# Node statistics and router sums on ScalarE and GpSimd inside the group stage, and the second MLP bias as one bf16 product

## The chip, the core and the metric

One NeuronCore of a Trainium2 chip runs the whole kernel. The metric is the device time of one launch in microseconds (us). The engines are named as the profile names them: PE is TensorE (PEld its weight loads), DVE is VectorE, ACT is ScalarE, POOL is GpSimd, SP is SyncE, which here only issues transfers. A name with q (POOLq) is the engine's instruction queue: loads of registers, branches, arithmetic on addresses.

## What is computed

One layer over a graph of 12500 nodes with 256 features each and 212500 edges:

```python
xn = _layernorm(x)
x = x + gnn(xn, weight, edge_weight, src, dst) + mix(xn, ...)
x = x + ffn(_layernorm(x), wr, br, w1, b1, w2, b2)

# gnn: out[src] += edge_weight * (xn @ weight)[dst]
# mix: linear attention over all nodes, x1 = layer_norm(t + xn) * g1 + b1n, then
#      h = gelu(x1 @ W1.T + b1);  y = h @ W2.T + b2;  layer_norm(y + x1) * g2 + b2n
# ffn: weights = x @ wr + br;  the 6249 nodes of largest weight:
#      y = (gelu(sel @ w1 + b1) @ w2 + b2) * weight, added to their rows
```

Two things of it matter here. The bias b2 of the mix's second matrix product (with the first layer norm's own bias added to it), and, between the two lines that set x, the mean and variance of each node's row and its product with wr, the router sum: without them no node can be normalised or chosen.

## The kernel before

The nodes are 98 tiles of 128 rows (NT = 98). The sum that becomes x stands in SBUF as `acc`, 256 columns to a tile. The edges come in 128 blocks of 1664 (NSB = 128).

In the main part, each block permutes and expands its edges on TensorE (L948 is the expansion, in bf16), ScalarE moves the result from PSUM to `rowbuf`, and GpSimd scatters it to DRAM, sorted by the tile that it is to be added to. Beside the blocks runs the mix: at first the attention's sums, and in later blocks the mixing of two tiles (49 times, in a pattern of two blocks with mixing and one without). Of one mixing, `mlp_down` is TensorE's last part: for each of two tiles the product with W2 (L1004, f32), x1 times a diagonal matrix (L1007), and the bias (L1009), then VectorE takes the statistics of the result (L1701). VectorE's step of a block begins at L1665, when TensorE has done the block before.

Then comes the group stage. The sorted rows are cut into groups of 256 that belong to one tile each, and tiles follow each other in order. A step has 8 groups (RG = 8), in four pairs k; 112 steps were made. For each pair SyncE loads its rows (L584), VectorE makes four one-hot matrices with the edge weights (L1822), TensorE multiplies them with the rows (L1082), ScalarE moves the sums to SBUF (L1341), and GpSimd adds them to the tile: it loads the tile's place from the row of group buckets (L725), waits for ScalarE and for its own last add (L726, L727), and adds (L728). Each buffer is given back by counting semaphores. The order on each engine is the order of the program.

Behind the last add stands the statistics loop: VectorE takes seven tiles at a time, their statistics (L1841), their product with wr into `prod` (L1843), and aggregates (L1848, L1850); ScalarE sums each product over its columns with an accumulator (L1348). Then VectorE works out the inverse square roots (`inv_sqrt`, from L1396), the router weights and the choice of nodes, and in the end comes the FFN over the chosen rows.

## Time and profile before

| | us |
|---|---|
| median of 3 runs | 3774.55 (3771.11 to 3775.57) |
| the profiled execution | 3799.59 |
| its span | 3797.8 |
| the stretch of mixing, by the bias products | 1284 to 2257 |
| the group stage's adds | 2354 to 3211 |
| the statistics loop | 3213 to 3291 |
| selection and FFN | from 3291 |

A profile is of one execution, and here that one took 0.7% longer than the median. Durations are read from it. The timeline gives the start, the length, engine, line and operation, what is written and read, how many follow each other, and in brackets how long the engine was idle before and what ended that. The chain is the sequence of work that ended last, followed back from the last instruction; a step is on it if the next one waited for it. An engine's busy share tells little where the stages have different limits: what a change in one stage is worth is read from the waits and the chain of that stage.

### The profile page before, as it was taken

To read this page: it belongs to the slowest core of one execution; us is meant where nothing else is said; L and a number is where in the kernel's file an instruction comes from. 1 tells how busy PE (TensorE), PEld (TensorE's weight loads), DVE (VectorE), ACT (ScalarE), POOL (GpSimd) and SP (SyncE) were. 2 spreads that over 40 slices of the span, in tenths; PEclk is the share of its full clock that TensorE was granted. 3 is DMA by queue.
4 is the path that set the end of the run, shared out by engine and by line. 5 is a ranking of instruction groups with operands and counts; after the bars stand their busy time and mean duration, and the time that the engine had idled before them with its cause. 6 is when DMAs were issued, how large, how long until landed. Compare 5 with 4: busy or idle time off the path is not lost.

```text
span 3797.8 us, 81728 instructions
## 1 busy us (share of the span) xinstructions
PE 3073.4 (81%) x18820; PEld 2305.1 (61%) x18820; DVE 2599.6 (68%) x6591; ACT 1555.3 (41%) x3781; POOL 2113.8 (56%) x2304
## 2 busy tenths in 40 slices
PE   3777738888888788888888886999999997029998
PEld 2444426666666666666676664777777775018887
DVE  6888884444444677777787773999999999861111
ACT  4444404555555444444444443333333333673222
POOL 1445534555555566666666565777777776003433
PEclk7899969999999999999899898999999999559999
DMA  5777727787777766666677666888888887161111
GB/s 162 239 262 261 256 73 239 263 261 254 252 264 262 237 229 217 216 215 222 222 228 231 203 211 221 272 278 276 277 276 277 277 277 229 62 217 50 54 52 44
DMA packets 427482, 818.33 MB, mean 215 GB/s; under 512 B 45499, under 2 KB 203191, under 8 KB 427256
## 3 DMA queue, kind: packets, MB, share of 16 engines
q1 hardware_dynamic: 348376, 559.80, 48.5%
q0 software_dynamic: 78880, 256.49, 17.7%
q14 instruction: 203, 1.66, 0.1%
q8 instruction: 23, 0.38, 0.0%
HBM read 459.96 MB, written 356.17 MB: 215 GB/s over the span
## 4 chain that ended last, share of the span: by engine, by line
PE 38%; issue 14%; DVE 14%; POOL 13%; ACT 6%; another core or an unknown queue 6%; DMA 3%; POOLq 3%; SPq 1%; DVEq 1%; ACTq 0%
POOL acc L728 13%; PE ps L948 12%; PE ps L1135 5%; PE ps L1125 5%; PE ps L961 3%; PE ps L995 2%; ACT rowbuf L1261 2%; POOLq L725 2%; PE ps L1082 2%; PE ps L1004 2%; DVE acc L1490 2%; PE ps L957 1%; DMA rowbuf<-sorted_rows 1%; DMA acc<-bucket_rows 1%
## 5 line engine op out<-in xcount | busy, mean ns | idle before, releaser
L695 POOL DMA_INDIRECT sorted_rows<-rowbuf,posu x896 | 1003.4, 1120 | 768.2 <-ACT rowbuf L1261 554.3
L948 PE MATMUL ps<-mainbuf 128*128 128x256 bf16 x5376 | 731.5, 280 | 195.7 <-ACT rowbuf L1261 140.5
L1082 PE MATMUL ps<-rowbuf,mainbuf 128*128 128x256 f32 x3584 | 844.7, 392 | 25.9 <-DVE mainbuf L1822 20.9
L1822 DVE TENSOR_SCALAR mainbuf<-cols,rowbuf 128x128 f32<-128x128 f32 x1792 | 820.9, 528 | 58.5 <-DMA rowbuf<-sorted_rows 50.2
L728 POOL TENSOR_TENSOR acc<-acc,node 128x256 f32 x896 | 673.3, 751 | 196.3 <-POOL acc L728 156.1
L1082 PEld LDWEIGHTS ps<-rowbuf,mainbuf 128*128 128x128 f32 x3584 | 620.3, 189 | 250.1 <-DVE mainbuf L1822 177.5
L948 PEld LDWEIGHTS ps<-mainbuf 128*128 128x128 bf16 x5376 | 502.2, 100 | 338.8 <-ACT rowbuf L1261 187.7
L1261 ACT ACTIVATE rowbuf<-ps 128x512 f32<-128x512 f32 x896 | 515.4, 594 | 447.2 <-PE ps L948 371.5
L1341 ACT ACTIVATE node<-ps 128x512 f32<-128x512 f32 x448 | 267.6, 597 | 603.0 <-PE ps L1082 499.4
L1665 DVE TENSOR_SCALAR mainbuf<-mainbuf,lane 128x1024 bf16<-128x1024 bf16 (+1 forms) x256 | 117.4, 458 | 254.4 <-PE ps L948 194.7
L1648 DVE TENSOR_TENSOR mainbuf<-tabs,cols 128x1664 bf16<-128x1664 f32 (+1 forms) x128 | 241.1, 1884 | 0.0
L1658 DVE TENSOR_REDUCE wl<-ps 128x14 f32<-128x28 f32 x128 | 24.1, 188 | 278.4 <-remote 245.0
L1331 ACT ACTIVATE rowbuf<-ps,fb_c 128x256 f32<-128x256 f32 x200 | 94.9, 474 | 253.7 <-PE ps L1125 245.2
L741 POOL DMA_INDIRECT acc<-sorted_rows,posu x50 | 48.6, 973 | 265.7 <-DVE posu L1963 197.3
L1252 ACT ACTIVATE wl<-ps 128x14 f32<-128x14 f32 x128 | 24.4, 190 | 407.8 <-DVE wl L1659 333.4
L961 PE MATMUL ps<-wqkvT,acc 128*128 128x512 f32 x392 | 185.5, 596 | 0.0
L852 PE MATMUL ps<-acc,mainbuf 128*128 128x416 f16 x512 | 125.4, 376 | 73.8 <-DVE acc L1490 73.8
L1135 PE MATMUL ps<-tabs,rowbuf 128*128 128x256 f32 x800 | 179.2, 382 | 5.4 <-ACT rowbuf L1331 5.1
L1125 PE MATMUL ps<-acc,tabs 128*128 128x256 f32 x800 | 179.3, 383 | 0.8 <-ACT acc L1326 0.8
L1135 PEld LDWEIGHTS ps<-tabs,rowbuf 128*128 128x128 f32 x800 | 149.9, 190 | 30.7 <-issue 9.6
L1651 DVE TENSOR_TENSOR mainbuf<-mainbuf,tabs 128x1092 bf16<-128x1092 bf16 x128 | 164.9, 1288 | 0.0
L1125 PEld LDWEIGHTS ps<-acc,tabs 128*128 128x128 f32 x800 | 146.0, 191 | 30.1 <-ACT acc L1326 1.2
(338 smaller groups left out, 4641.1 us busy)
## 6 DMA issues: line engine op xcount, KB each, us to landing
rowbuf<-sorted_rows SPq DMA_DIRECT2D x448, 516.0 KB, 4.5
mainbuf<-slot_rows_in_window SPq DMA_DIRECT2D x128, 448.0 KB
acc<-bucket_rows SPq DMA_DIRECT2D x128, 416.0 KB, 6.1
sorted_rows<-node SPq DMA_DIRECT2D x105, 258.0 KB, 2.4
mainbuf<-support_rows SPq DMA_DIRECT2D x128, 192.0 KB
sorted_rows<-rowbuf,posu POOLq DMA_INDIRECT x896
node<-in_x SPq DMA_DIRECT2D x104, 128.0 KB, 5.1
sorted_rows<-rowbuf SPq DMA_DIRECT2D x14, 903.0 KB, 4.9
```

Source lines behind the costliest of these rows:

```text
L695: g.indirect_dma_start(pairs_d, bass.IndirectOffsetOnAxis(posu[:, PC * k + c:PC * k + c + 1], 0), rowbuf[:, S * k + 2 * c:S * k + 2 * c + ...
L728: g.tensor_tensor(acc[:, ds(at, C)], acc[:, ds(at, C)], sums[:, k, h * C:(h + 1) * C], ALU.add).then_inc(acc_done, 1)
L948: last = mm(ps[:, MSG + (k + c) % 2, u * C:(u + 1) * C], oht[:, s * P:(s + 1) * P], win[:, k, v * C:(v + 1) * C], start=v == 0, stop=v == 2)
L961: last = mm(ps[:, KVPS + u, :], xnT_b[u][:, c * P:(c + 1) * P], wqkvT[:, c, C:3 * C], start=c == 0, stop=c == CC - 1)
L1082: last = mm(ps[:, GRP + k, h * C:(h + 1) * C], ohw[:, k % 2, s * P:(s + 1) * P], rowbuf[:, BT * k + s, 0:C], start=t == 0, stop=t == 1)
L1125: last = mm(ps[:, 2 + m % 2, 0:C], fw1_s[:, c, m * P:(m + 1) * P], x3T[:, s, c * 2 * P:(c + 1) * 2 * P], start=c == 0, stop=c == CC - 1)
L1135: last = mm(ps[:, 4 + s, u * C:(u + 1) * C], fhT[:, s, m, u * P:(u + 1) * P], fw2_s[:, m, :], start=m == 0, stop=m == HID // P - 1)
L1261: A(rowbuf[:, S * k + 2 * c:S * k + 2 * c + 2, 0:C], ps[:, MSG + (k + c) % 2, :].rearrange("p (t c) -> p t c", t=2), ACT.Copy).then_inc(ro ...
L1341: A(sums[:, k, :], ps[:, GRP + k, :], ACT.Copy).then_inc(sums_ready, 1)
L1648: v.tensor_tensor(ohp, pA[:, :, ds(i, 1)].to_broadcast([P, T, P]), cols[:, :].unsqueeze(1).to_broadcast([P, T, P]), ALU.is_equal).then_inc ...
L1651: v.tensor_tensor(rhs, ohs.unsqueeze(3).to_broadcast([P, T, S, V]), metab[:, ds(i, 1), :, :].rearrange("p a t v -> p (a t) v").unsqueeze(2 ...
L1822: v.tensor_scalar(ohw[:, k % 2, s * P:(s + 1) * P], cols[:, :], rowbuf[:, r, C + 1:C + 2], rowbuf[:, r, C:C + 1], ALU.is_equal, ALU.mult). ...
```

## The change

Each step of the group stage now also handles one finished tile, by a table of turns. Before the stage, VectorE works out the table (`turn_row`) from the group buckets: for each step the next tile whose groups are all in steps before; where there is none, the last one is done again. After the last step a loop goes on until all 98 tiles have had their turn. In a step, GpSimd waits until all adds of the step before are done, loads the tile's number and multiplies the tile with wr. ScalarE has four operations between its evictions: a sum over the tile's columns, its negative mean, a sum of squares about the mean, and the sum of GpSimd's product. The statistics loop is gone; VectorE waits for the last turn and makes two small operations of it. Apart from that, b2 is split by VectorE at the start of the kernel into three bf16 parts, which stand in partitions 0, 32 and 64 of a tile of zeros, and the bias product multiplies ones with all 128 partitions of it in bf16, in place of one partition in f32.

```diff
+        b2_parts = sb("b2_parts", [P, C], BF16)
...
-        prod = rowflat[:, 0:2 * GC].rearrange("p (s t c) -> p s t c", s=2, t=G)
+        NTURN = NGMAX // RG + 1 + NT
+        turn_of, turn_q, turn_one = (mb[0:1, 4900 + k * NTURN:4900 + (k + 1) * NTURN] for k in range(3))
+        turn_row = mb[0:1, 4900 + 3 * NTURN:4900 + 4 * NTURN].bitcast(I32)
+        prod, dump = part(2048, C, of=node), part(2304, C, of=node)
+        sum1, mean_n, sum2 = part(4500, NT, of=mb), part(4600, NT, of=mb), newt_t[:, 2, :]
...
+            pool.wait_ge(w2_in, 32)
+            pool.wait_ge(norm_set, 1)
+            turns = pool.value_load(tki[0:1, 6:7], min_val=2, max_val=NTURN)
+
+            def router(i):
+
+                c = pool.value_load(turn_row[0:1, ds(i, 1)], min_val=0, max_val=NT - 1)
+                pool.wait_ge(stat_done, 4 * i + STAT0)
+                pool.sem_inc(passed, 1)
+                g.tensor_tensor(prod, acc[:, ds(c * C, C)], vec2[:, WR, :], ALU.mult).then_inc(prod_ready, 1)
+
             with pool.Fori(0, steps) as i:
+                pool.wait_ge(acc_done, ACC0 + RG * i)
+                router(i)
...
+            pool.wait_ge(acc_done, ACC0 + RG * steps)
+            pool.sem_inc(passed, 1)
+            with pool.Fori(steps, turns) as i:
+                router(i)
...
-                    last = mm(ps[:, YPS, u * C:(u + 1) * C], onesf[0:1, :], vec[0:1, B2, :], start=False, stop=True)
+                    last = mm(ps[:, YPS, u * C:(u + 1) * C], ones_b[:, :], b2_parts[:, :], start=False, stop=True)
...
+            act.wait_ge(norm_set, 1)
+            turns = act.value_load(tki[0:1, 6:7], min_val=2, max_val=NTURN)
+
+            def stat(i, c, k):
+
+                if k > 0 and k < 3:
+                    act.wait_ge(stat_done, 4 * i + STAT0 + k)
+                if k == 0:
+                    A(dump, acc[:, ds(c * C, C)], ACT.Copy, accum_out=sum1[:, ds(c, 1)]).then_inc(stat_done, 1)
+                if k == 1:
+                    A(mean_n[:, ds(c, 1)], sum1[:, ds(c, 1)], ACT.Copy, scale=-1.0 / C).then_inc(stat_done, 1)
+                if k == 2:
+                    A(dump, acc[:, ds(c * C, C)], ACT.Square, bias=mean_n[:, ds(c, 1)],
+                      accum_out=sum2[:, ds(c, 1)]).then_inc(stat_done, 1)
+                if k == 3:
+                    act.wait_ge(prod_ready, i + 1)
+                    A(prod, prod, ACT.Copy, accum_out=wts[:, ds(c, 1)]).then_inc(stat_done, 1)
+
             with act.Fori(0, steps) as i:
+                c = act.value_load(turn_row[0:1, ds(i, 1)], min_val=0, max_val=NT - 1)
                 for k in range(KB):
                     act.wait_ge(grp_mm, GRP0 + RG * i + 2 * k + 2)
                     act.wait_ge(acc_done, RG * i + 2 * k + 2)
                     A(sums[:, k, :], ps[:, GRP + k, :], ACT.Copy).then_inc(sums_ready, 1)
-
-
-            with act.Fori(0, NG // 2) as i:
-                for s in range(2):
-                    act.wait_ge(prod_ready, 2 * i + s + 1)
-                    for t in range(G):
-                        A(prod[:, s, t, :], prod[:, s, t, :], ACT.Copy,
-                          accum_out=wts[:, ds(2 * G * i + G * s + t, 1)]).then_inc(prod_read, 1)
+                    if k == 0:
+                        act.wait_ge(acc_done, ACC0 + RG * i)
+                    stat(i, c, k)
+            act.wait_ge(acc_done, ACC0 + RG * steps)
+            act.sem_inc(passed, 1)
+            with act.Fori(steps, turns) as i:
+                c = act.value_load(turn_row[0:1, ds(i, 1)], min_val=0, max_val=NT - 1)
+                for k in range(4):
+                    stat(i, c, k)
...
-            chain.inc(v.tensor_tensor(vec[0:1, B2, :], vec[0:1, B2, :], vec[0:1, DIAG, :], ALU.add))
+            chain.inc(v.tensor_tensor(vec[:, B2, :], vec[:, B2, :], vec[:, DIAG, :], ALU.add))
+            chain.inc(v.memset(b2_parts[:, :], 0.0))
             chain.wait()
+
+            for k in range(3):
+                b_, r_ = b2_parts[32 * k:32 * k + 1, :], vec[32 * k:32 * k + 1, B2, :]
+                for _ in range(k):
+                    v_link(v.tensor_copy(b_, r_))
+                    v_link(v.tensor_tensor(r_, r_, b_, ALU.subtract))
+                v_link(v.tensor_copy(b_, r_))
...
+            NST = NGMAX // RG + 1
+            dve.wait_ge(gb_in, 16)
+            chain.inc(v.tensor_copy(tk[0:1, 7:8], meta[0:1, 1:2]))
+            chain.inc(v.memset(turn_one, 1.0))
+            chain.inc(v.memset(turn_of[:, NST:NTURN], float(NT)))
+            v_link(v.tensor_copy(turn_of[:, 0:NST], gb_row[0:1, 1:1 + RG * NST].rearrange("a (i k) -> a i k", k=RG)[:, :, 0]))
+            chain.inc(v.tensor_scalar(turn_of[:, 0:NST], turn_of[:, 0:NST], 1.0 / C, None, ALU.mult))
+            v_link(v.tensor_scalar(turn_q[:, 0:NST], cols[0:1, 0:NST], tk[0:1, 7:8], float(NT), ALU.is_ge, ALU.mult))
+            v_link(v.tensor_tensor(turn_of[:, 0:NST], turn_of[:, 0:NST], turn_q[:, 0:NST], ALU.add))
+            v_link(v.tensor_scalar(turn_of, turn_of, float(NT), None, ALU.min))
+            v_link(v.tensor_tensor_scan(turn_q, turn_one, turn_of, 0.0, ALU.add, ALU.min))
+            chain.inc(v.tensor_scalar(turn_of, turn_q, 1.0, float(NT), ALU.is_lt, ALU.mult))
+            v_link(v.tensor_scalar(turn_one, turn_q, float(NT), None, ALU.is_ge))
+            chain.inc(v.tensor_reduce(tk[0:1, 7:8], turn_one, AX.X, ALU.add))
+            chain.inc(v.scalar_tensor_tensor(turn_row, turn_q, -1.0, turn_of, ALU.add, ALU.add))
+            chain.wait()
+            v_link(v.tensor_scalar(tki[0:1, 6:7], tk[0:1, 7:8], -1.0, float(NTURN + 1), ALU.mult, ALU.add))
+            v.sem_inc(norm_set, 1)
...
-            wr_ = vec2[:, WR:WR + 1, :].to_broadcast([P, G, C])
-            with dve.Fori(0, NG // 2) as i:
-                chain.enter(i, 2 * (2 * G + 1))
-                for s in range(2):
-                    n = 2 * i + s
-                    for t in range(G):
-                        chain.inc(v.bn_stats(stats[:, t, :], acc[:, ds(n * GC + t * C, C)]))
-                    dve.wait_ge(prod_read, G * (n + 1))
-                    v.tensor_tensor(prod[:, s, :, :], acc[:, ds(n * GC, GC)].rearrange("p (t c) -> p t c", t=G), wr_,
-                                    ALU.mult).then_inc(prod_ready, 1)
-                    chain.wait()
-                    dve.sem_inc(passed, 1)
-                    for t in range(G):
-                        chain.inc(v.bn_aggr(mvs[:, t, :], stats[:, t, :]))
-                    chain.wait()
-                    v_link(v.tensor_copy(mv[:, ds(G * n, G), :], mvs[:, :, :]))
-            chain.leave(NG // 2)
-            dve.wait_ge(prod_read, PROD0 + NT)
+            turns = dve.value_load(tki[0:1, 6:7], min_val=2, max_val=NTURN)
+            dve.wait_ge(stat_done, 4 * turns + STAT0)
+            dve.sem_inc(passed, 1)
+            chain.inc(v.tensor_scalar(mv[:, :, 0], mean_n, -1.0, None, ALU.mult))
+            v_link(v.tensor_scalar(mv[:, :, 1], sum2, 1.0 / C, None, ALU.mult))
             inv_sqrt(mv[:, :, 1], rstd[:, :], newt_t[:, 0, :], newt_t[:, 1, :])
```

## Rows read from the trace of the kernel before

**Rows 1.** The page, part 4: the chain that ended last, shares of the span by line.

```profile
POOL acc L728 13%; PE ps L948 12%; PE ps L1135 5%; PE ps L1125 5%; PE ps L961 3%; PE ps L995 2%; ACT rowbuf L1261 2%; POOLq L725 2%; PE ps L1082 2%; PE ps L1004 2%; DVE acc L1490 2%; PE ps L957 1%; DMA rowbuf<-sorted_rows 1%; DMA acc<-bucket_rows 1%
```

**Rows 2.** Waits, 2500 to 3200 us: who waited <- for whom: us in total, times, longest.

```profile
ACT node L1341 <- PE ps L1082: 409.0, 307, 2.1
...
ACT node L1341 <- POOL acc L728: 72.2, 60, 2.0
...
POOL acc L728 <- ACT node L1341: 21.5, 126, 0.2
```

**Rows 3.** Timeline of a group step: start us, us, engine, line, op, idle before it.

```profile
2806.98 0.74 POOL L728 TENSOR_TENSOR acc<-acc,node 128x256 f32 x1 [0.45 <-POOL acc L728]
...
2807.89 0.73 POOL L728 TENSOR_TENSOR acc<-acc,node 128x256 f32 x1 [0.17 <-POOL acc L728]
...
2814.62 0.72 POOL L728 TENSOR_TENSOR acc<-acc,node 128x256 f32 x1 [0.46 <-POOL acc L728]
```

**Rows 4.** The chain in order of time over a step boundary: start us, us, what.

```profile
2704.54 0.74 POOL acc L728
...
2705.30 0.04 POOLq L728
...
2706.37 0.07 POOL acc L728
...
2706.72 0.28 POOLq L725
...
2707.58 0.71 POOL acc L728
```

**Rows 5.** Timeline: VectorE before the group stage, its first add and its last.

```profile
2348.92 0.35 DVE L1822 TENSOR_SCALAR mainbuf<-cols,rowbuf 128x128 f32<-128x128 f32 x1 [21.14 <-DMA rowbuf<-sorted_rows]
...
2354.09 0.75 POOL L728 TENSOR_TENSOR acc<-acc,node 128x256 f32 x1 [12.11 <-ACT node L1341]
...
3210.90 0.72 POOL L728 TENSOR_TENSOR acc<-acc,node 128x256 f32 x1 [0.20 <-POOL acc L728]
```

**Rows 6.** Timeline of the statistics loop: its first pieces, and what follows it.

```profile
3215.34 2.02 DVE L1843 TENSOR_TENSOR rowbuf<-acc,mainbuf 128x1792 f32<-128x1792 f32 x1
...
3217.51 0.42 ACT L1348 ACTIVATE rowbuf<-rowbuf 128x256 f32<-128x256 f32 x1 [8.83 <-DVE rowbuf L1843]
3217.83 0.19 ACT L1348 ACTIVATION_READ_ACCUMULATOR rowbuf<-rowbuf  x1
...
3290.95 0.21 DVE L1396 TENSOR_SCALAR mainbuf<-mainbuf 128x98 f32<-128x98 f32 x1 [2.23 <-ACT rowbuf L1348]
```

**Rows 7.** The chain, 1284 to 2257 us (the mixing of nodes): shares by line.

```profile
by line: issue 20.1%; PE ps L948 19.9%; PE ps L995 8.8%; another core or an unknown queue 7.0%; PE ps L1004 7.0%; PE ps L1009 4.6%; DVE stats L1701 3.6%; PE ps L1007 3.3%; ACT rowbuf L1261 3.1%; DVE acc L1753 2.3%; DVE mainbuf L1651 1.9%; D
```

**Rows 8.** Timeline of TensorE in one mixing block.

```profile
1784.61 1.03 PE L1004 MATMUL ps<-wqkvT,node 128*128 128x256 f32 x4
1785.48 0.61 PE L1007 MATMUL ps<-vec,node 128*128 128x128 f32 x4
1786.01 0.69 PE L1009 MATMUL ps<-vec,onesf 1*128 1x256 f32 x2
1786.64 1.13 PE L1004 MATMUL ps<-wqkvT,node 128*128 128x256 f32 x4
...
1788.77 1.48 PE L948 MATMUL ps<-mainbuf 128*128 128x256 bf16 x12
1790.09 0.66 PE L919 MATMUL ps<-mainbuf 128*128 128x84 bf16 x13
```

**Rows 9.** Timeline of VectorE around the same block, from one L1665 to the next.

```profile
1776.73 0.42 DVE L1665 TENSOR_SCALAR mainbuf<-mainbuf,lane 128x768 bf16<-128x768 bf16 x1 [1.71 <-PE ps L948]
...
1790.91 0.41 DVE L1665 TENSOR_SCALAR mainbuf<-mainbuf,lane 128x768 bf16<-128x768 bf16 x1
```

**Rows 10.** Timeline of VectorE after the preparation of weights at the start.

```profile
34.37 0.65 DVE L1461 TENSOR_SCALAR acc<-acc,lane 128x1664 f16<-128x1664 f16 x1 [4.30 <-DMA acc<-bucket_rows]
```

**Rows 11.** VectorE line L1822 alone: durations of one, and who waited for it.

```profile
L1822 DVE TENSOR_SCALAR mainbuf<-cols,rowbuf x1792: 332/346/907, 2348.9 to 3206.5; 128x128 f32<-128x128 f32 x200
```

More of the change, by code:

```diff
@@ L314, in gps_layer_kernel @@
             "rows_ready", "norm_set", "xid_ready", "idu_ready", "fo_out", "fo_free"))
-        prod_ready, prod_read = sem("prod_ready"), sem("prod_read")
+        prod_ready, stat_done = sem("prod_ready"), sem("stat_done")
         x3_out = [sem(f"x3_out{s}") for s in range(2)]
@@ L327, in gps_layer_kernel @@
         XT0, FH0 = 1, 2
-        TREAD0, FO0, PROD0 = 2, 2, 2 * G
+        TREAD0, FO0, STAT0 = 2, 2, 4
         TAB = 6 + 16
@@ L1167, in _ @@
             act.sem_inc(sums_ready, SUM0)
-            act.sem_inc(prod_read, PROD0)
+            act.sem_inc(stat_done, STAT0)
             wq = [wqkvT[:, 0, 0:512], wqkvT[:, 0, 512:768], wqkvT[:, 1, 0:512], wqkvT[:, 1, 512:768],
@@ L1364, in tail_rows @@
                       scale=twice[:, ds(G * n + t, 1)], bias=minus[:, ds(G * n + t, 1)]).then_inc(rows_ready, 1)
-            act.wait_ge(norm_set, 3)
+            act.wait_ge(norm_set, 4)
             for s in range(2):
```

## Prediction

> **What bounds the kernel now.** I read the page's list of lines on the chain first, then the waits and the timeline of the stage that the change enters, then its chain in order of time, then the stretch of mixing. One line leads the whole chain: GpSimd's add of a group's sums, 13% of the span, with 2% more for its own load of the bucket number [rows 1]. That is the group stage. In the waits of that stage ScalarE waits for TensorE most of the time (so it has room), and 60 times for GpSimd's adds, while GpSimd waits for ScalarE 126 times for 21.5 us in all, 0.2 us at most [rows 2]. So GpSimd is what the stage runs at: an add follows the one before at 0.91 us, of which 0.17 is the pause for its own semaphore, and at the boundary of a step the pause is 0.45. From one boundary to the next it is 2814.62 - 2806.98 = 7.64 us [rows 3]. The boundary itself shows why: within a step the queue fetches the next bucket number while an add runs; across the branch it can't. The last add of a step starts at 2706.37, the load at 2706.72, the next add at 2707.58, so that this pitch is 1.21 instead of 0.91, and 0.86 us lie between the start of a load and the start of the work that needs it [rows 4]. The stage's adds start from 2354.09 to 3210.90: 856.8 us, or 111 steps of 7.66 and a rest of 6.4 for the last seven pitches [rows 5]. Behind it the statistics loop stands alone until 3290.95 [rows 6]. In the mixing before, TensorE alternates on the chain with VectorE, with 4.6% of 973 us at the bias product L1009 [rows 7].
>
> **Part 1, GpSimd's router product in each step (dearer).** The diff puts at the head of each of the 112 steps: a wait for the last add of the step before, a load of the turn's tile, a wait for ScalarE's four statistics, and one product of 128x256. Its shape and operands are the add's, so I take the add's 0.75 us [rows 3]. The wait stands before the load, so nothing of the load hides any more: the last add runs 0.75, some 0.04 go until the queue moves on (2704.54 + 0.74 to 2705.30 [rows 4]), then 0.86 from load to product: the product starts 1.65 us after the last add. While it runs, the queue fetches the first bucket number; those 0.86 us and 0.05 of dispatch are longer than the product's 0.75, so the first add comes 0.91 later. Add to add over the boundary is 2.56 us instead of 1.21: 1.35 more. I take off 0.08: one threshold fewer to work out than at the old boundary, and the small hold-ups of the old stage (7.66 against 7.64) lose their cause when the others wait for GpSimd. That is 1.27 x 111 = **141 us more**. The ends: if the queue hid all but the product, 0.75 x 111 = 83; if sem_inc and the waits cost another quarter of a microsecond, 1.6 x 111 = 178. I stay near the upper working, since it is put together from pieces of the same queue. The first step's product is free: it can run in the 12.11 us in which GpSimd waits before its first add [rows 5].
>
> **Who waits for that.** Behind GpSimd's new waits are only its own adds. ScalarE gets four operations a step: two activations of 256 with accumulator (0.42 and a read of 0.19 that starts 0.32 later [rows 6]) over acc, one over the product, and one of a single column, between 0.19 and 0.42. Its four evictions take 2.4 us a step: 700 us less 409.0 and 72.2 of waiting [rows 2] are 219 in 91.6 steps. Together that is some 4.3 us in a step of 8.9. Its wait for the last add sits before the second eviction; that eviction is there about 1.2 us after the last add, and GpSimd needs it only 2.56 + 1.8 us after the start of that add: no stall. VectorE, TensorE and the loads (SyncE issues them when TensorE has used a buffer) get 1.27 us more slack per step.
>
> **Part 2, the table of turns.** Some 14 small operations on one partition, on VectorE before the stage, and a load that all three engines make. VectorE is idle for 21.14 us there [rows 5], for the first rows from DRAM, and the group buckets that the table needs are fetched ahead of these: 0, at most 3 us if that cover were gone. The groups go by at 8 a step and there are 98 tiles in 112 steps, so the turns keep up and one is left over, two at most.
>
> **Part 3, the statistics loop goes (gain).** From the last add's start to the first operation behind the loop are 3290.95 - 3210.90 = 80.1 us [rows 5, 6]. What is left of it: the last add, 0.75; loop entry and load on ScalarE, about 0.8; three activations with accumulator of 0.5, a column of 0.25 and three handshakes, 2.0; two small operations on VectorE, 0.5. That is 4.1 us, **76 less**; 73 if two turns are left. The loop's own pace needs no looking into: it goes whole (a product of 2.02 us for seven tiles on VectorE, and ScalarE's sums [rows 6]).
>
> The row says that VectorE makes this product at 2.02 / 7 = 0.29 us a tile, and GpSimd's add takes 0.75. The Trainium skill (GPSIMD Engine Reference, introduction) calls GpSimd the wrong choice for ordinary elementwise work and VectorE roughly twice as fast; by that factor the product would be 0.58, but the sum stays, as the queue's 0.91 is longer than either.
>
> **Part 4, the bias product (gain).** L1009 multiplies one partition in f32; after, all 128 in bf16. Between the start of L1004 and that of L948 lie 4.16 us for two tiles [rows 8]. In one tile the four L1004 take 0.87 and four L1007 of half the width half of that, 0.44: 1.31. The bf16 product has the shape of L948's: twelve of these take 1.32, so 0.11 [rows 8]. After the change two tiles take 2 x 1.42 = 2.84, so 1.32 less per block, and 49 blocks give 65 us of TensorE. How much is on the path: 4.6% of 973 is 44.8 us, and the chain gives 0.62 to a product (1786.01 to 1786.64), so 72 of 98 lie on it. But in the block shown VectorE runs from L1665 at 1776.73 to that at 1790.91 without waiting, 14.2 us, as long as TensorE [rows 9]: where two such blocks follow each other, VectorE is next in line at once, and the second saves little. In the first, VectorE had waited 1.71 us for TensorE, more than 1.32, so that one saves in full. The kernel's loop puts two blocks with mixing and one without in turn, so about 25 of the 49 are first ones: they give 33, the rest 0.3 each: **40 less**. The ends are 20 and 65.
> Splitting b2 adds nine short chained operations on VectorE, at most 4 us, ahead of a wait of 4.30 us for bucket rows [rows 10]: 0.
>
> **Sum.** 141 - 76 - 40 = 25 us more. Against the profiled execution (span 3797.8, time 3799.59) that is 3824.6; the median of the unprofiled runs is 3774.55, 0.7% below it, and the same 25 us give 3799.6. I say 3800 us.
>
> **Rivals.**
> *Faster: the queue hides the turn's load.* The product costs a step only what one more add does, 0.92 us: 102 us. With 76 and 40 back it is 3774.55 - 14 = 3760, with the full 65 it is 3736. It decides for faster once the extra per step is below (76 + 40) / 111 = 1.05 us. For it: within a step the load does hide. Against: the wait stands before the load. Chance 0.15.
> *Slower: the bias gain is lost* to VectorE and the scatters of the mixing: 141 - 76 = +65, 3840. For it: rows 9. Against: the wait of 1.71 us in front. Chance 0.12.
> *ScalarE becomes late for GpSimd.* Its statistics, all behind the wait for the last add, delay the second pair's sums; at 0.4 a step 44 us, 3844. Against: 4.3 us of work in 8.9. Chance 0.05.
> *VectorE is held out while GpSimd works.* Its one-hots take 0.346 at the median and up to 0.907 [rows 11], so some stand still behind GpSimd. Two pass per add and pause; sixteen are needed. With nine operations and a boundary of 0.9 us free there are more such openings, not fewer. If one more round of 0.92 were needed in two steps of three: +68, 3868. Chance 0.05. The Trainium skill (GPSIMD Engine Reference, Specifications) has the SBUF interfaces shared with VectorE, which is this mechanism.
> *The change doesn't do what it says:* the table falls behind and leaves a dozen tiles for after the stage, 2.8 us each: +31, 3831. Chance 0.03. The forecast keeps 0.60, and its own spread is 3775 to 3825.
>
> **Chances and range.** About 0.2%, 7.5 us, is what a measurement of this kernel tells from no change: 3767 to 3782. Faster: the first rival but for its upper edge, 0.15. Within: the low side of the forecast with the bias gain near its full size, 0.14. Slower: 0.71. The range, 3758 to 3842, takes in the better half of the first rival and the lost bias gain.
>
> **What would show it.** Right: add to add over a step's boundary 2.4 to 2.7 us, steps of 8.9, GpSimd first on the chain with about 17%, ScalarE's waits for GpSimd up and TensorE's for VectorE down; from the last add to the first inv_sqrt operation 4 us; one product of 0.11 where L1009 stood, and the blocks of mixing in sum 30 to 50 us shorter. Wrong: boundaries below 2.3 us, or a mixing stretch that keeps its length.

## The result and the profile after

The changed kernel takes 3833.54 us (median of 4 runs, 3832.59 to 3836.68); the kernel before, beside it on the same chip, 3772.98 (4 runs, 3771.11 to 3775.57). The ratio is 1.0158, interval 1.0142 to 1.0174: 60.6 us slower. The profiled execution of after took 3832.59 us with a span of 3830.8.

The page of the kernel after: busy time of the engines, the chain by line, then groups (instruction, count | busy us, mean ns | idle before it). GpSimd's add is L746 here, its router product L735, ScalarE's evictions L1382, its statistics L1367 to L1375, VectorE's one-hots L1893.

```profile
span 3830.8 us, 83999 instructions
...
PE 3046.4 (80%) x18722; PEld 2362.1 (62%) x18722; DVE 2468.5 (64%) x6393; ACT 1644.7 (43%) x4377; POOL 2179.1 (57%) x2417
...
POOL acc L746 9%; PE ps L970 9%; PE ps L1104 9%; PE ps L1157 5%; PE ps L1147 5%; PE ps L983 3%; DMA rowbuf<-sorted_rows 2%; DVE acc L1532 2%; ACT rowbuf L1283 2%; PE ps L979 2%; DVE mainbuf L1701 1%; DVE stats L1751 1%; ACT node L1382 1%; PE ps L893 1%
...
L1893 DVE TENSOR_SCALAR mainbuf<-cols,rowbuf 128x128 f32<-128x128 f32 x1792 | 757.1, 484 | 257.6 <-PE ps L1104 139.1
```

Timeline of GpSimd over one boundary of the group stage, kernel after (start us, us, engine, line, op, idle before it). It answers to [rows 3, 4].

```profile
2906.90 0.75 POOL L746 TENSOR_TENSOR acc<-acc,node 128x256 f32 x1 [0.17 <-POOL acc L746]
2908.64 0.73 POOL L735 TENSOR_TENSOR node<-acc,mainbuf 128x256 f32<-128x256 f32 x1 [0.98 <-ACT node L1367]
2909.53 0.76 POOL L746 TENSOR_TENSOR acc<-acc,node 128x256 f32 x1 [0.17 <-ACT node L1382]
2910.47 0.76 POOL L746 TENSOR_TENSOR acc<-acc,node 128x256 f32 x1 [0.17 <-ACT node L1382]
```

Call this the boundary: from the last add of a step to the first of the next it is 2909.53 - 2906.90 = 2.63 us. The product starts 1.74 after the last add and the next add 0.89 after the product. Over all steps the median boundary is 2.618 (before: 1.198), the median pitch from add to add inside a step 0.923 (before: 0.924), the median step 9.067 (before: 7.634).

Waits of the same stage, 2500 to 3200 us, kernel after (who <- for whom: us in total, times, longest); they answer to [rows 2].

```profile
ACT node L1367 <- POOL acc L746: 390.4, 77, 5.2
PEld ps L1104 <- DVE mainbuf L1893: 142.1, 140, 2.4
DVE mainbuf L1893 <- PE ps L1104: 100.8, 102, 3.9
```

ScalarE now stands 5 us in every step at the statistics' wait for the last add: 390.4 us in 77 steps, where its largest wait was one of 409.0 for TensorE [rows 2]. The timeline puts the product's wait down to ScalarE's L1367, but by the program it waits only for the statistics of the step before. The left-over turn at the end of the stage shows it: its product L735 starts at 3326.15, and L1367 of the same turn at 3326.21.

The end of the stage, kernel after: last add, the left-over turn, and VectorE's first operations behind it. It answers to [rows 5, 6].

```profile
3324.26 0.72 POOL L746 TENSOR_TENSOR acc<-acc,node 128x256 f32 x1 [0.17 <-POOL acc L746]
...
3326.21 0.42 ACT L1367 ACTIVATE node<-acc 128x256 f32 x1 [7.02 <-issue]
...
3328.34 0.21 DVE L1909 TENSOR_SCALAR mainbuf<-mainbuf 128x98 f32<-128x98 f32 x1 [2.20 <-ACT node L1375]
...
3328.70 0.21 DVE L1438 TENSOR_SCALAR mainbuf<-mainbuf 128x98 f32<-128x98 f32 x1
```

Where the time went, by stages, from the starts of the instructions that bound them. The kernel before stands twice: the execution that the prediction read, and a later one from the chip of set 1 (below).

| stage, us | before, as read | before, again | after | after less again |
|---|---|---|---|---|
| blocks without nodes (49) | 686.9 | 678.2 | 675.1 | -3.1 |
| first to last bias product | 972.9 | 959.4 | 942.9 | -16.4 |
| last bias product to first add | 97.2 | 97.4 | 96.7 | -0.7 |
| first to last add | 856.8 | 859.6 | 1015.2 | +155.6 |
| last add to inv_sqrt | 80.0 | 80.0 | 4.4 | -75.6 |
| inv_sqrt to the FFN | 125.8 | 125.8 | 121.8 | -4.0 |

With the short stretches left out here the last column adds up to the difference of the spans, 3830.8 - 3777.3 = 53.5. Beside the execution that was read, after is 33.0 longer; from median to median it is 60.6. The execution that was read was a long one of its kernel, by 8.7 + 13.5 us in the blocks and the mixing, as the first two columns show.

The last row is no work of the change. Choosing the nodes is a loop of 16 turns on VectorE, and before its first operation (L1885 in before, L1943 in after) VectorE is idle for 13.2 us in all in before, 8.9 in after, 9.3 with the bias product alone and 9.3 with the short roots alone (set 4 below). The loop's own code is the same in all of them; what sets the pause is open. So each of these versions starts with some 4 us less, whatever it changes.

### The profile page after: what moved, and what is told of

Same layout as the page of the kernel before. It is cut to its first block, busy times and chain, and to the rows that moved or that the text cites. A ratio compares the mean times of both kernels' runs of the same rounds, so it can differ in the third digit from the quotient of the medians.

```text
span 3830.8 us, 83999 instructions
## 1 busy us (share of the span) xinstructions
PE 3046.4 (80%) x18722; PEld 2362.1 (62%) x18722; DVE 2468.5 (64%) x6393; ACT 1644.7 (43%) x4377; POOL 2179.1 (57%) x2417
## 3 DMA queue, kind: packets, MB, share of 16 engines
q14 instruction: 202, 1.65, 0.2%
## 4 chain that ended last, share of the span: by engine, by line
PE 39%; DVE 20%; issue 13%; POOL 10%; ACT 7%; another core or an unknown queue 4%; DMA 4%; POOLq 1%; DVEq 1%; SPq 1%; ACTq 1%
POOL acc L746 9%; PE ps L970 9%; PE ps L1104 9%; PE ps L1157 5%; PE ps L1147 5%; PE ps L983 3%; DMA rowbuf<-sorted_rows 2%; DVE acc L1532 2%; ACT rowbuf L1283 2%; PE ps L979 2%; DVE mainbuf L1701 1%; DVE stats L1751 1%; ACT node L1382 1%; PE ps L893 1%
## 5 line engine op out<-in xcount | busy, mean ns | idle before, releaser
L700 POOL DMA_INDIRECT sorted_rows<-rowbuf,posu x896 | 988.6, 1103 | 739.0 <-ACT rowbuf L1283 501.9
L1104 PE MATMUL ps<-rowbuf,mainbuf 128*128 128x256 f32 x3584 | 878.3, 405 | 145.8 <-ACT node L1382 89.2
L1893 DVE TENSOR_SCALAR mainbuf<-cols,rowbuf 128x128 f32<-128x128 f32 x1792 | 757.1, 484 | 257.6 <-PE ps L1104 139.1
L1104 PEld LDWEIGHTS ps<-rowbuf,mainbuf 128*128 128x128 f32 x3584 | 702.8, 201 | 321.2 <-DVE mainbuf L1893 209.5
L746 POOL TENSOR_TENSOR acc<-acc,node 128x256 f32 x896 | 669.0, 747 | 162.9 <-POOL acc L746 118.6
L1382 ACT ACTIVATE node<-ps 128x512 f32<-128x512 f32 x448 | 262.4, 587 | 74.6 <-POOL acc L746 52.1
L1367 ACT ACTIVATE node<-acc 128x256 f32 x113 | 47.0, 416 | 561.1 <-POOL acc L746 554.1
```

Of the source, the lines that this page charges most:

```text
L700: g.indirect_dma_start(pairs_d, bass.IndirectOffsetOnAxis(posu[:, PC * k + c:PC * k + c + 1], 0), rowbuf[:, S * k + 2 * c:S * k + 2 * c + ...
L746: g.tensor_tensor(acc[:, ds(at, C)], acc[:, ds(at, C)], sums[:, k, h * C:(h + 1) * C], ALU.add).then_inc(acc_done, 1)
L1104: last = mm(ps[:, GRP + k, h * C:(h + 1) * C], ohw[:, k % 2, s * P:(s + 1) * P], rowbuf[:, BT * k + s, 0:C], start=t == 0, stop=t == 1)
L1382: A(sums[:, k, :], ps[:, GRP + k, :], ACT.Copy).then_inc(sums_ready, 1)
L1893: v.tensor_scalar(ohw[:, k % 2, s * P:(s + 1) * P], cols[:, :], rowbuf[:, r, C + 1:C + 2], rowbuf[:, r, C:C + 1], ALU.is_equal, ALU.mult). ...
```

## The experiments

Each set ran on one chip and has its own runs of the kernel before: set 1, 3774.96 us (11 runs), set 2, 3631.67 (9), set 3, 3794.37 (11), set 4, 3631.81 (9). Ratios are against those. Differences in us are of medians, and they can differ by some us from what the ratio gives.

**Set 1: the parts apart.** Only the hunks on b2:

```diff
-                    last = mm(ps[:, YPS, u * C:(u + 1) * C], onesf[0:1, :], vec[0:1, B2, :], start=False, stop=True)
+                    last = mm(ps[:, YPS, u * C:(u + 1) * C], ones_b[:, :], b2_parts[:, :], start=False, stop=True)
```

> Before, with the bf16 bias product and its three parts alone. Theory that the bias gain is about half of what was forecast, since VectorE is next in line in the blocks of mixing: 20 to 25 us faster, 3750. Rival, the forecast's own term: 40 us faster, 3733. Rival that no gain comes at all: 3773. The group stage must stay at 857 us.

Measured: 3761.14, ratio 0.9968 (0.9957 to 0.9979), -14 us: less than either value expected, and more than none. In the profiles the stretch from the first to the last bias product is 12 us shorter (959.4 to 947.5). Everything but those hunks:

> Before, with the statistics and router sums moved into the group stage alone (bias as before). From the stages of the profiles: group stage 158 us longer, statistics 76 us shorter, so 82 us slower, 3855. If the parts add up, this and the bias alone give the 60.6 us of both. Rival: the group stage costs more in unprofiled executions than in the profile, then 100 us slower with the bias worth 40.

Measured: 3855.09, ratio 1.0211 (1.0197 to 1.0225), +80 us. Its stage of adds is 1014.5 us and its rest behind the last add 4.4: 158 longer and 76 shorter than the rows that were read, 82 together. So the group stage and the statistics explain all of +80. The two parts sum to 80 - 14 = +66 beside the +60.6 of the whole; the 5 us between them are not explained.

The router's load moved ahead of its wait for the last add:

```diff
+                c = pool.value_load(turn_row[0:1, ds(i, 1)], min_val=0, max_val=NT - 1)
                 pool.wait_ge(acc_done, ACC0 + RG * i)
-                c = pool.value_load(turn_row[0:1, ds(i, 1)], min_val=0, max_val=NT - 1)
```

> The changed kernel, with GpSimd's load of the turn's tile placed ahead of its wait for the last add. In the changed kernel the load starts 0.87 us after the last add's start and the product 1.74 us after it. Theory: the load then runs while the last add does, the product starts 1.15 to 1.25 us after it, a step is 0.5 us shorter, 50 to 60 us in all: about 3778. Rival: the step is set by the engine's own work and not by its queue, then less than 10 us are gained.

Measured: 3795.25, ratio 1.0049 (1.0034 to 1.0064), +20: some 40 us better than the changed kernel's +60.6. Its GpSimd over a boundary:

```profile
2701.23 0.74 POOL L746 TENSOR_TENSOR acc<-acc,node 128x256 f32 x1 [0.17 <-POOL acc L746]
2702.53 0.73 POOL L736 TENSOR_TENSOR node<-acc,mainbuf 128x256 f32<-128x256 f32 x1 [0.56 <-POOL acc L746]
2703.44 0.84 POOL L746 TENSOR_TENSOR acc<-acc,node 128x256 f32 x1 [0.18 <-issue]
```

And its chain over another boundary, in order of time (POOLq is GpSimd's queue):

```profile
2709.99 0.07 POOL acc L746
...
2710.33 0.29 POOLq L732
...
2711.32 0.33 POOL node L736
...
2712.21 0.75 POOL acc L746
```

The product now starts 1.30 after the last add (1.74 with the load behind the wait), the median boundary is 2.203, and the stage of adds 968.9, so 46 us less. The load L732 starts at 2710.33, 0.34 after the add has, and runs beside it; yet the product starts only at 2711.32. The queue's work from load to start takes 0.99 there by itself and sticks out behind the add. So the load can be hidden beside the add, but what the queue does from the load to the product is longer than the add. The product was expected 1.15 to 1.25 us after the last add and came after 1.30; of the 50 to 60 us expected the stage gave 46 and the whole some 40. The rival, that the engine's own work sets the step and less than 10 us are gained, falls.

**Set 2: what the mixing is bound by, and the statistics without GpSimd.** In the factors of the node blocks, inverse roots with one Newton round instead of three (so these roots are less exact), without and with the new bias product:

```diff
-                inv_sqrt(mvs[:, a:a + n, 1], rs[:, a:a + n], newt[:, 0, a:a + n], newt[:, 1, a:a + n])
+                inv_sqrt(mvs[:, a:a + n, 1], rs[:, a:a + n], newt[:, 0, a:a + n], newt[:, 1, a:a + n], rounds=1)
```

> Before, with one Newton round in place of three in the layer norms of the mixing blocks (their results are less exact): six operations of 0.2 us fewer, 1.2 us of VectorE per mixing block, 59 us in all; the bias product as before. Theory that TensorE's bias product and VectorE's chain are both near the limit there: alone it gives little, 10 to 20 us, since TensorE is then what a block waits for: 3755 to 3765. Rival, VectorE is the limit already: 40 us or more.

Measured: 3579.37, ratio 0.9844 (0.9825 to 0.9862), -52. That is the rival's value: most of the 59 us that VectorE no longer works reach the end (some 4 of the 52 are the shorter pauses of the choosing loop), so on this chip it was at the limit already and not behind TensorE.

> The same shorter VectorE chain with the bf16 bias product. Theory that the bias gain of the change was cut from 40 to 13 us because VectorE was next in line: with VectorE's chain 1.2 us shorter the bias product is worth 30 us or more against the run with one Newton round alone: about 3725. Rival, the scatters to DRAM are next in line and not VectorE: again some 13 us, about 3748.

Measured: 3571.29, ratio 0.9821 (0.9803 to 0.9838): only 8 below the run above, where the VectorE theory wanted 30 or more and its rival some 13. The bias product taken out (the second bias isn't added):

> Before without any second bias product (b2 is left out of the result), so TensorE saves another 0.11 us per tile and all the gaps around the product. Theory (VectorE next in line): no more than 3 us better than the bf16 product: about 3758. Rival (the forecast's sum was right in kind, the bf16 product costs more than 0.11 us): clearly below 3750.

Measured: 3615.36, ratio 0.9949 (0.9932 to 0.9967), -16. With the bf16 product it is -14 and -20 on other chips (sets 1 and 4), so that product costs next to nothing itself.

No product on GpSimd: three statistics in ScalarE's turns, and the router sums in a loop of seven tiles behind the stage, as before the change:

```diff
-                g.tensor_tensor(prod, acc[:, ds(c * C, C)], vec2[:, WR, :], ALU.mult).then_inc(prod_ready, 1)
...
+                    v.tensor_tensor(prod[:, s, :, :], acc[:, ds(n * GC, GC)].rearrange("p (t c) -> p t c", t=G), wr_,
+                                    ALU.mult).then_inc(prod_ready, 1)
```

> The changed kernel with no product on GpSimd: ScalarE takes the statistics in the group stage; the products with wr (VectorE, seven tiles at 2.01 us) and their sums (ScalarE, seven at 0.40) come in a loop behind the stage. Theory (GpSimd's queue and product are the whole cost of the group stage, ScalarE's statistics are free): group stage back to 857 to 862 us, then 14 x 2.9 + 3 = 44 us in place of 80: 3773 - 13 - 36 = 3724, and faster than both kernels. Rival (ScalarE's waits in the stage cost too): steps of 8.0 or more, 3760.

Measured: 3579.82, ratio 0.9845 (0.9828 to 0.9861), -52. Its stage of adds is 857.0 us, as long as before the change, and the stretch to inv_sqrt 44.9 instead of 80.0. ScalarE's statistics inside the stage are free; the 158 us come from GpSimd's product and the waits and the load in front of it.

**Set 3: the product on VectorE, and the price of the bias product.** The product moved to VectorE, ahead of the one-hots of the last buffer of a step:

```diff
+                c = dve.value_load(turn_row[0:1, ds(i, 1)], min_val=0, max_val=NT - 1)
...
+                    if k == KB - 1:
+                        dve.wait_ge(acc_done, ACC0 + RG * i)
+                        router(i, c)
```

> The changed kernel with the router product made by VectorE (128x256 f32, about 0.41 us) before the fourth pair's one-hots of each step, in place of GpSimd. Theory (the cost was GpSimd's queue and product; VectorE has 0.3 to 0.5 us free in each step): steps of 7.7 to 8.0 us in place of 9.07, 77 us less than the changed kernel at least behind them: 60 to 95 us faster than before. Rival (VectorE is kept out by GpSimd's adds, so one more operation costs a whole add, 0.92): steps of 8.5.

Measured: 3726.16, ratio 0.9815 (0.9789 to 0.9842), -68: the fastest version of set 3, ahead of both kernels of the case. VectorE's product and GpSimd's adds around a boundary in it, from two timelines:

```profile
2707.42 0.41 DVE L1876 TENSOR_TENSOR node<-acc,mainbuf 128x256 f32<-128x256 f32 x1
...
2705.48 0.75 POOL L733 TENSOR_TENSOR acc<-acc,node 128x256 f32 x1 [0.17 <-ACT node L1365]
2706.67 0.74 POOL L733 TENSOR_TENSOR acc<-acc,node 128x256 f32 x1 [0.44 <-POOL acc L733]
```

The boundary is back at 1.19. The stage of adds is 866.2 us, 11.6 above the kernel before in this set (854.6), and the 75.6 behind it are kept.

The f32 bias product issued twice (the second bias is added twice):

```diff
+                    mm(ps[:, YPS, u * C:(u + 1) * C], onesf[0:1, :], vec[0:1, B2, :], start=False, stop=False)
                     last = mm(ps[:, YPS, u * C:(u + 1) * C], onesf[0:1, :], vec[0:1, B2, :], start=False, stop=True)
```

> Before with the f32 bias product made twice (b2 counts double in the result), so TensorE has 0.62 to 0.66 us more per tile, 61 to 65 us in all. Forecast's view (three of four such products lie on the path): 45 us slower. Theory (the path passes from TensorE to others as soon as TensorE gets shorter, but not when it gets longer): 40 us or more slower, though taking the same time away gave 13. Rival (other waits hide TensorE's time either way): some 13 us slower.

Measured: 3828.82, ratio 1.0078 (1.0048 to 1.0107), +34 by the medians and +30 by the ratio: short of the 40 or more of the theory, and well above the 13 of the rival. And a bf16 product over one partition instead of 128 (only the first part of the second bias is added):

```diff
+                    last = mm(ps[:, YPS, u * C:(u + 1) * C], ones_b[0:1, :], b2_parts[0:1, :], start=False, stop=True)
```

> The bf16 bias product from one partition in place of 128 (two of b2's three parts are left out, so the result is less exact). If the time around the old product comes from reading one partition, L1004 to L948 takes 2 x (1.31 + 0.11) plus two stops of 0.2 to 0.4 us each: 3.3 us or more. If it comes from f32 alone, 2.84 us as with 128 partitions.

Measured: 3782.16 (one run). The interval from the start of the first L1004 of a block to the first L948 behind the bias products is the same in all 49 blocks of each kernel, but for one block of 9.56 in the run with the product twice: 4.16 us in before, 5.02 with the product twice, 3.33 with one bf16 row, 2.84 with 128 rows, 2.62 without it. TensorE's timeline in the run with one row, then in the one with the product twice:

```profile
1722.01 0.28 PE L1010 MATMUL ps<-b_parts,ones_b 1*128 1x256 bf16 x1
1722.22 1.13 PE L1005 MATMUL ps<-wqkvT,node 128*128 128x256 f32 x4
```
```profile
1710.27 0.69 PE L1009 MATMUL ps<-vec,onesf 1*128 1x256 f32 x2
1710.81 0.59 PE L1010 MATMUL ps<-vec,onesf 1*128 1x256 f32 x2
1711.33 1.13 PE L1004 MATMUL ps<-wqkvT,node 128*128 128x256 f32 x4
```

**Set 4: the four cells on one chip.** The bias product alone, the short roots alone, and both, since the runs of sets 1 and 2 came from chips that differ in these very blocks.

> The kernel before with the bias product alone in bf16 parts, in one set with the two runs beside it, so that the four cells (bias product old or new, VectorE's inverse roots in the node blocks long or short) stand on one chip. VectorE theory (VectorE takes over at once when the bias product is shorter): 10 to 15 us below the kernel before, and much more than that with the short roots. Row-traffic theory (gathers and scatters of rows of the same blocks are what comes next): about 10 below here and about the same with the short roots.

Measured: 3611.47, ratio 0.9940 (0.9927 to 0.9954), -20.

> The kernel before with one Newton round in place of more in the factors of the node blocks (so these inverse roots are less exact), some 59 us less of VectorE. Both theories: 40 to 60 us below the kernel before, as in the first look.

Measured: 3574.88, ratio 0.9857 (0.9835 to 0.9878), -57.

> Short roots (less exact, as beside) and the bias product in bf16 parts together. VectorE theory: with VectorE relieved the bias product is worth 30 us or more, so at least 30 below the run with short roots alone. Row-traffic theory: 5 to 15 below it, no more than the bias product is worth alone.

Measured: 3572.49, ratio 0.9835 (0.9822 to 0.9849), -59. With VectorE relieved the bias product gives 2 us by the medians, 8 by the ratios (and 8 in set 2), not 30; alone it gives 20. Some 4 us of the 20, of the 57 and of the 59 are the shorter pauses of the choosing loop. The theory that VectorE's time hid the bias gain falls. First the waits of the run with the short roots and the new product, 1300 to 2100 us, then its chain over that stretch:

```profile
DVE posf L1678 <- POOLq L702: 68.3, 30, 7.4
```
```profile
by line: issue 24.2%; PE ps L949 11.5%; DMA sorted_rows<-rowbuf,posu 6.7%; POOL sorted_rows L696 5.3%; PE ps L996 5.2%; DVE stats L1710 4.6%; PE ps L1005 3.9%; DVE mainbuf L1660 3.4%; ACT rowbuf L1262 3.3%; DVE acc L1762 2.9%; DVE mainbuf L
```

The same view of the run with the new product alone, set 4:

```profile
by line: issue 26.7%; PE ps L949 9.0%; DVE mainbuf L1660 6.9%; DVE stats L1710 6.3%; DVE wqkvT L1738 4.1%; DVE newt L1402 3.8%; DVE rs L1403 3.5%; DVE newt L1401 3.4%; DVE acc L1762 3.2%; DVE mainbuf L1674 3.1%; DVE mvs L1714 2.6%; DVE wqkv
```

With the bias product alone the chain runs through VectorE's factors (L1401 to L1403, L1710). With the roots short as well, scatters of rows (L696, and their transfers of 5 to 7 us) stand on it with 12%, and VectorE waits for them 68.3 us. So the path of a block runs through VectorE's factors first of all: 59 us less work there gave 57 (53 without the choosing loop's 4), and 65 us less on TensorE gave 20 alone and 2 to 8 beside the short roots. That the scatters are what limits the stretch once both are shorter is read from these views; no run took them away.

**Where the bias gain goes, block by block.** The starts of TensorE's first expansion product (L948 and its like) give the length of every block. These are the 51st to the 127th block, among them all with mixing, in mean us for one block:

| | before, set 1 | new product, set 1 | before, set 3 | product twice, set 3 |
|---|---|---|---|---|
| with mixing, the first after one without (23) | 19.53 | 17.31 | 19.55 | 20.77 |
| with mixing, behind another such (26) | 12.77 | 12.98 | 12.76 | 13.55 |
| without mixing (28) | 9.16 | 10.30 | 9.28 | 8.93 |
| all 77 | 1037.7 | 1023.9 | 1041.3 | 1080.2 |

The two columns of before show how well such a mean repeats. The first blocks gain 2.2 us each, 51 in all, which is more than the 1.32 that TensorE no longer works. The blocks behind them lose 0.2 each, 5 in all, and the blocks without mixing lose 1.1 each, 32 in all: 14 are left. The whole change beside set 1's run without its bias part shows the same, -2.5, +0.2 and +1.3. The waits tell who takes the time back: TensorE waits longer for ScalarE's evictions, and ScalarE longer for a release that the profile can't name ("remote"; 63.1 us where it was 30.3). By the program that is most likely the row buffer, which is free when its scatter has landed; no run shows this. Waits, 1300 to 2100 us, set 1, before, then with the new product:

```profile
PE ps L948 <- ACT rowbuf L1261: 46.1, 51, 2.9
```
```profile
ACT rowbuf L1262 <- remote: 63.1, 34, 3.6
PE ps L949 <- ACT rowbuf L1262: 62.1, 65, 2.6
```

## Why the prediction was right or wrong

The direction and the list of parts were right and the time is inside the range, but the forecast was 25 us more and 60.6 were measured. The bias product's gain was 26 us too large and GpSimd's product 17 too small. Point by point:

**GpSimd's product, the largest term: 141 predicted, 158 measured.** The mechanism is as written: nothing of the load hides behind the wait, and the rival in which the queue hides it falls (boundary 2.62, where it needed about 2.1). Two pieces of the sum were off, and this is the smaller failed step. The product starts 1.74 after the last add instead of 1.65; the 0.09 lies between the end of the add and the start of the load, for which the sum had 0.04. And the 0.08 "I take off" for a threshold and small hold-ups was not there: the add starts 0.89 after the product, as the pieces said, and the steps scatter as little as before (nine in ten lie within some 0.2 us in both). 1.42 per boundary instead of 1.27, over 111 steps, is 158. The discount was the one number of the term without a row.

**ScalarE and VectorE: no cost, as predicted.** ScalarE's waits changed from TensorE to GpSimd, and with the product gone and its statistics kept the stage was 857.0 us. The rivals with a late ScalarE and a VectorE held out had no part: the pitch inside a step stayed at 0.92, and VectorE's one-hots took 0.345 us at the median and 0.902 at most, as before (0.346 and 0.907 [rows 11]). That GpSimd would lead the chain with about 17% was wrong: it shows 9%, as much as TensorE's L1104. The steady pitches, and a boundary that moved with GpSimd's load alone, are the surer reading of what the stage runs at. The followed-back chain takes the release that came last, even by a tenth of a microsecond: at 2909.53 it leaves GpSimd for ScalarE's eviction L1382, although the add comes 0.89 after the product in every step.

**The table: nothing.** From the last scatter to the first add it is 14.2 us in after and 14.1 in before. One turn is left over, as counted.

**The statistics: 76 predicted, 75.6 measured** (80.0 to 4.4). This is the row whose pieces were all in the trace.

**The bias product: 40 predicted, 14 measured (20 on the chip of set 4).** This is the step that failed. Its first half, the TensorE time, was exact: 2.84 us for two tiles, and 65 us of TensorE less. Its second half was not: a fifth to a third of the 65 us reaches the end. "About 25 of the 49 are first ones: they give 33, the rest 0.3 each" looked at the blocks with mixing alone. There are 23 first ones, and they gained even more than was said, 51 us; the second ones gained nothing (0.2 lost each), near what was said. What the sum put at nothing, without a reason, is the third block of the pattern, the one without mixing: it grew by 1.1 us each and took 32 back. TensorE's and ScalarE's waits there grew with it; what is behind them stays open. Nor was VectorE "next in line": on the chips of sets 2 and 4, relieving it gave most of its time, so it was on the path before the change. The other direction isn't the same number: 0.86 us a block more, 42 in all, cost 34. The rival "the bias gain is lost to VectorE and the scatters", with a chance of 0.12, named the right kind of loss and came nearest with +65. That it came so near is in part luck, for it kept the 141 of GpSimd, 17 too low, and put the gain at 0, 14 too low.

**The sum.** With the measured terms it is 158 - 76 - 14 = 68, against 60.6. The 8 us between them are not explained by a term. Single profiles of one kernel differ by as much: the three of before have 856.8, 859.6 and 854.6 us in the stage of adds and 972.9, 959.4 and 962.3 in the mixing. The 4 us of the choosing loop are in the 14 already, since the run with the bias product alone has them too.

**The basis.** "The same 25 us" against the profiled execution and the median was a sound rule, but the profiled execution was 22 us long in just the two stages where the bias product's gain was read. Against it the changed kernel is 33 longer, which looks like the 25 and isn't; against a second profile of before on the chip of set 1 it is 53.5. The two errors of the forecast, 17 and 26, both point the same way.

## What to carry to other kernels

Price work that goes onto the leading queue by its whole path at the wait: end of the last operation, the wait passed, the register load, the dispatch; let no discount stand without a row. The same product cost 158 us on GpSimd behind its own wait and 12 on VectorE, which had the room, and moving one load ahead of the wait gave some 40 back. Where the path of a stretch changes between engines, relief of one may be worth a fraction of its time (here 14 to 20 of 65 us), and its share of the chain is no measure of it. Count the whole pattern of blocks, those without the changed work too: the time gained in one was taken back in the next. And a second profile of the same kernel shows how far a stage's length can be trusted.

## What the runs showed of the hardware

**One partition costs more than 128.** From the intervals above, one bf16 product of 256 columns over 128 partitions costs (2.84 - 2.62) / 2 = 0.11 us, the same over one partition (3.33 - 2.62) / 2 = 0.36. In f32 the first one-partition product costs (4.16 - 2.62) / 2 = 0.77 and a second one directly behind it (5.02 - 4.16) / 2 = 0.43. So about 0.25 to 0.34 us of a one-partition product between full ones isn't its columns but the change to one partition and back. The weight loads show where: with 128 partitions the load for the bias product starts 0.11 us ahead of the product itself (1662.07 and 1662.18, bias product alone, set 1). With one partition both start at 1722.01, and those of the next L1005 both at 1722.22. So neither load runs ahead of its product. The Trainium skill (TensorEngine Tiling (Array Packing), Key Properties) says that a change of the tiling mode drains the engine; the loads that no longer run ahead agree with such a drain, but whether the engine changed its mode here no run shows.

**GpSimd and VectorE on the same product.** 128x256 in f32 takes 0.73 us on GpSimd (L735 in after) and 0.41 on VectorE (L1876 in the run with the product there); the 0.29 a tile of [rows 6] holds only for the seven tiles of one instruction. The Trainium skill (GPSIMD Engine Reference, introduction) has VectorE roughly twice as fast on elementwise work; 1.8 here agrees. Of the 1.42 us that a step grew, only half is the operation's own time.

**Chips differ, in the blocks.** The kernel before takes 3775 and 3794 us on the chips of sets 1 and 3, and 3632 on those of sets 2 and 4. The group stage and all behind it agree within some us; the blocks don't. One stretch of blocks, 600 to 1100 us, the same instructions in the kernel before (set 1) and in the one with short roots (set 4), which are not in this stretch yet (engine by engine busy us and count, then granted clock, DMA share, GB/s):

```profile
600.00:1100.00 500.00, 436.38 (x3535) 324.03 (x3535) 244.80 (x592) 268.56 (x778) 283.70 (x259) 1.00 0.81 264
```
```profile
600.00:1100.00 500.00, 491.17 (x4067) 378.26 (x4065) 291.20 (x678) 329.28 (x890) 345.73 (x297) 1.00 0.90 301
```

Both at the full granted clock, the second moves 301 GB/s instead of 264 and gets 297 operations of GpSimd done instead of 259. Who waits there differs too: GpSimd's scatters for ScalarE 162.7 us in the first and 70.2 in the second. The work itself isn't shorter: the mean operation of GpSimd takes 1.10 us in the first and 1.16 in the second, and the transfers move 326 and 334 GB/s for each share of their engines that is busy (264 / 0.81 and 301 / 0.90). So it is the waits that differ; what makes them longer on one chip, the traces don't tell. The bias part of this change was worth 14 us on one chip and 20 on another.
